# Third attention: the weighted products of two steps issued together

## What is computed

```python
q = (query @ Wq).reshape(b, sq, 32, 16).transpose(0, 2, 1, 3)
k = jnp.repeat((key @ Wk).reshape(b, sk, 8, 16).transpose(0, 2, 1, 3), 4, axis=1)
v = jnp.repeat((value @ Wv).reshape(b, sk, 8, 16).transpose(0, 2, 1, 3), 4, axis=1)
scores = jnp.einsum('bhqd,bhkd->bhqk', q, k) * 16 ** -0.5
probs = jax.nn.softmax(scores, axis=-1)
out = jnp.einsum('bhqk,bhkd->bhqd', probs, v)
x = x + jnp.tanh(g_xattn[2]) * (out.transpose(0, 2, 1, 3).reshape(b, sq, 512) @ Wo)
```

## Time and profile before

| | us |
|---|---|
| median of 3 runs | 1259.44 |
| lowest, highest | 1258.63, 1262.66 |
| profiled execution | 1258.08 |
| its span (first to last instruction) | 1256.3 |
| loop of the third attention (step 0 to last product) | 952.2 to 1058.9 of the span |

### The profile page before, as it was taken

How to read it: one execution, slowest core, us unless ns; L and a number is a source line. 1 busy time by engine, 2 the same in 40 slices (tenths; PEclk the granted TensorE clock), 3 DMA queues, 4 the chain that set the end, 5 groups by cost and what they waited for, 6 DMA issues and landing times.

```text
span 1256.3 us, 19440 instructions
## 1 busy us (share of the span) xinstructions
PE 1182.3 (94%) x7154; PEld 927.8 (74%) x7154; DVE 909.4 (72%) x1748; ACT 637.6 (51%) x1046; POOL 517.5 (41%) x385
## 2 busy tenths in 40 slices
PE   6999999999999998999989999997899998999986
PEld 5878888878888876777878879886775444777733
DVE  6589888886798798874677976897557773442287
ACT  3466556645566555641355644565146777232252
POOL 5126365625236377534242724234634002265212
PEclk9999999999999999999999999999999999999999
DMA  5588869975689597850386956878131000572000
GB/s 193 104 157 162 170 140 179 181 142 107 137 157 185 123 179 137 158 136 22 72 167 109 219 97 120 165 132 174 37 123 25 1 2 1 166 168 76 1 1 34
DMA packets 356238, 146.39 MB, mean 117 GB/s; under 512 B 327793, under 2 KB 334097, under 8 KB 356145
## 3 DMA queue, kind: packets, MB, share of 16 engines
q1 hardware_dynamic: 356144, 145.15, 55.3%
HBM read 57.17 MB, written 5.37 MB: 50 GB/s over the span
## 4 chain that ended last, share of the span: by engine, by line
PE 48%; DVE 9%; ACT 2%; POOL 2%; issue 2%; DMA 1%; SPq 0%; DVEq 0%; ACTq 0%; POOLq 0%
PE ps L876 6%; PE ps L2018 5%; PE ps L904 4%; PE ps L843 4%; PE ps L1584 3%; PE ps L1610 3%; DVE p L1166 3%; DVE rows_and_turned L1152 3%; PE ps L828 2%; PE ps L2031 2%; PE ps L819 2%; PE ps L805 2%; PE ps L2316 2%; PE ps L1566 1%; PE ps L1595 1%
## 5 line engine op out<-in xcount | busy, mean ns | idle before, releaser
L1000 ACT ACTIVATE ps<-ps,rows_and_turned 128x768 f32<-128x768 f32 x192 | 168.1, 875 | 201.5 <-DVE rows_and_turned L1152 201.5
L876 PE MATMUL ps<-kT,qT 128*128 128x512 f32 (+3 forms) x1152 | 238.9, 343 | 27.8 <-DVE p L1166 26.3
L876 PEld LDWEIGHTS ps<-kT,qT 128*128 128x128 f32 (+1 forms) x1152 | 199.2, 189 | 83.0 <-DVE p L1166 29.7
L1008 ACT ACTIVATE p<-ps,rows_and_turned 128x768 f16<-128x768 f32 x192 | 173.0, 901 | 125.2 <-ACT ps L1000 114.3
L904 PE MATMUL ps<-pT,vv 128*128 128x256 f16 (+1 forms) x1728 | 221.7, 274 | 6.2 <-issue 6.2
L1152 DVE TENSOR_REDUCE rows_and_turned<-ps 128x1 f32<-128x768 f32 x192 | 183.1, 954 | 56.8 <-PE ps L876 54.9
L1166 DVE SCALAR_TENSOR_TENSOR p<-ps,rows_and_turned,p 128x768 f16<-128x768 f32 (+2 forms) x256 | 201.4, 808 | 3.7 <-ACT p L1008 3.7
L904 PEld LDWEIGHTS ps<-pT,vv 128*128 128x128 f16 (+1 forms) x1728 | 167.3, 107 | 26.5 <-issue 9.6
L828 PE MATMUL ps<-xT,wq 128*128 128x512 f32 x528 | 144.0, 408 | 0.0
L737 POOL TENSOR_TENSOR wo<-raw,one 128x512 fp32r<-128x512 f32 (+1 forms) x48 | 50.8, 1058 | 225.2 <-PE ps L843 199.4
L1942 POOL TENSOR_TENSOR f2w<-f2raw,f2w 128x1024 fp32r<-128x1024 f32 (+2 forms) x33 | 52.6, 1622 | 149.2 <-ACT f2w L2062 149.2
(11 more groups left out here) (277 smaller groups left out, 1913.9 us busy)
## 6 DMA issues: line engine op xcount, KB each, us to landing
raw<-in_l_wq SPq DMA_DIRECT2D x44, 256.0 KB, 3.3
f2raw<-in_f_w SPq DMA_DIRECT2D x11, 776.0 KB, 5.0
rows_and_turned<-in_m_w SPq DMA_DIRECT2D x11, 768.0 KB, 5.6
raw<-in_l_wo SPq DMA_DIRECT2D x32, 256.0 KB, 3.3
pT<-p SPq DMA_TRANSPOSE x192, 3.7
raw<-in_l_wo SPq DMA_DIRECT2D x16, 192.0 KB, 3.3
w3gu<-rows_and_turned SPq DMA_DIRECT2D x11, 256.0 KB, 2.8
ctxraw<-in_ctxT SPq DMA_DIRECT2D x2, 1024.0 KB, 8.0
```

The lines of the kernel that those rows point to most:

```text
L876: last = nc.tensor.matmul(sc[:, lo:hi], query(A, h, qp)[:, r * P:(r + 1) * P], keys(A, h // A.g)[0:hd, kp, b, lo:hi], start=(qp, kp) == PA ...
L1000: nc.scalar.activation(score_banks(n), score_banks(n), ACT.Exp, bias=nmax[:, n % 32:n % 32 + 1], accum_out=rsum[:, n % 32:n % 32 + 1]).the ...
L1008: nc.scalar.activation(p16[:, n % 3, HI], score_banks(n), ACT.Copy, scale=rden[:, n % 32:n % 32 + 1]).then_inc(sem("att_half"), 1)
```

## The change

In odd steps no product is issued any more. In an even step n, from 2 on, both `weighted(n - 2)` and `weighted(n - 1)` are issued, one behind the other. The last two products, behind the loop, stay as they are, and so do the queues of all other engines, the buffers and the semaphores.

```diff
@@ -1673,8 +1673,9 @@
                     shifted(g + 1, 1, "l2_q4", 2 * g + 3)
                 if i == 7 and g + 2 < G2:
                     queries(g + 2, 1, "l2_q4", 2 * g + 4)
-                if n >= 2:
+                if n >= 2 and n % 2 == 0:
                     weighted(n - 2)
+                    weighted(n - 1)
             weighted(STEPS2 - 2)
             weighted(STEPS2 - 1)
             rows(G2 - 1, "l2_rows", G2 - 1)
```

## The result

| | before | changed |
|---|---|---|
| median of 22 runs each, us | 1260.74 | 1265.44 |
| span of the profiled execution, us | 1256.3 | 1264.6 |
| loop: first load of step 0 to first load of the last product | 952.18 to 1058.18 = 106.0 | 953.94 to 1065.59 = 111.65 |

The ratio is 1.0044, with a 95% interval of 1.0033 to 1.0054: 5.5 us slower, between 4.2 and 6.8; the two medians lie 4.7 apart. The loop alone is 5.65 us longer; the forecast was 5.8.

What follows compares the result with a forecast made beforehand. The prediction took the round trip of the two score banks as the bound, not TensorE's work. Terms of +3.2, +1.5, +0.6 and +0.5 made +5.8 us on the median 1259.44: 1265.2 us, range 1261.0 to 1269.5.

Steps and rivals of the forecast that it cites:

- first rival: TensorE's work is the bound: each of 31 pairs saves 0.14, nothing is given back, 1255.1 us; 6 in 100.
- empty step: Odd step i = 5, without product or tile: TensorE stands idle, the step lasting 1.35 us.
- round trip: A score's wait for its bank's earlier reduction: 0.54 + 0.69 + 0.12 = 1.35 us.
- Step (1): Product behind its neighbour in even steps: the second costs 0.43 instead of 0.57 us, a pair 1.00.
- third rival: Products don't stream in the loop, 0.57 + 0.57: 29 x 0.14 = 4.1 us more, 1269.3; 11 in 100.
- Step (2): Odd steps without a product: 1.35 us each, from start to start, with or without a tile.
- second rival: Odd steps' idle time comes back in even ones: 1259.4 us, or 1258 to 1261; 9 in 100.
- Step (3): Even steps, second score 0.59 late: 2.02 us at i = 0 and 2, 2.61 at 6, 2.81 at 4.
- wait for the output rows at i = 4: Tile at i = 4 waits for VectorE's output rows of i = 3, ending at 2.44: 0.20 us more.
- Step (4): Products' waits for exponentials: none while scores run, before step 53.
- output copy: ScalarE's copy holding up a group's first product: can start sooner, which gains nothing.
- saved switch: TensorE's saved change to another kind of tile, 0.14 us a pair; decides where no score waits for its bank.

Runs made afterwards that it cites:

- halved reductions: Reductions read 256 of 512 columns, in both kernels: kernel before 1249.57 us, changed kernel 1258.88 us, one run each, beside 1262.11 for the kernel before.
- the pairs in odd steps: Against the changed kernel, both products (n-3 and n-2) issued in odd steps, none in even ones: 1267.89 us, ratio 1.0062 to the kernel before.
- the product put back: Changed kernel with the pair of i = 4 undone, one product each at i = 4 and i = 5: 1265.63 us, one run.
- the moved products: Against the kernel before, products moved from steps that turn a tile to steps that don't, up to three in one: 1256.09 us, ratio 0.9972.

## Why the prediction was right

**The bound.** The argument that carried it was that a step costs the same with and without a product. Read by the busy share alone, would have given the first rival, and a gain. Halving the reductions confirms it: the engine with 21.0 us of idle time was part of the path. The changed kernel's empty step shows that it is there by the round trip (1.34, and 1.07 with halved reductions), not by its share of work.

**The number.** That the median came out at 1265.44 for a forecast of 1265.2 is in part luck. The forecast added 5.8 to a median of three runs, 1259.44; over 22 runs the kernel before has 1260.74. What can be held against the 5.8 is the loop's 5.65 and the ratio's 5.5.

**Step (1), the pair.** 1.00 from the pair's first load to the next score's, as the single pair at the end had shown. The third rival (no streaming behind a held score) is refuted by the row at 991.40 and its successor. It was priced at 29 pairs, without a word on which; 26 stand in steps with scores, and these would give 3.6 more instead of 4.1.

**Step (2), odd steps.** 1.34 with and without a tile, forecast 1.35. The second rival, that the hole is filled, is refuted by the empty step of 1.34 and by the pairs in odd steps.

**Step (3), even steps.** 2.02, 2.81, 2.61, 2.03 as forecast. The wait for the output rows at i = 4 was foreseen from VectorE's own order. Its multiplication is here:

```profile
1005.10 0.42 DVE L1814 TENSOR_TENSOR rows_and_turned<-ps,rden 128x256 f32<-128x256 f32 x1
```

It ends 2.44 into step 27 (1003.08), the number worked out.

**Step (4), waits.** While scores run, a product waited for an exponential only by what the view shows as 0.17 ahead of 991.40, which is the gap it also has where nothing holds it (996.24 to 996.83); the exponential of step 19, which that pair needs, had ended at 990.05. The output copy cost the step at i = 2 nothing beyond 0.01.

**The sum**, part by part:

| | forecast | loop of the trace |
|---|---|---|
| steps 2 to 8 | +1.5 | 13.03 - 11.54 = +1.5 |
| steps 9 to 48 | +3.2 | 74.16 - 71.04 = +3.1 |
| steps 49 to 52 | +0.6 | 7.53 - 6.92 = +0.6 |
| steps 53 to 63 | +0.5 | 13.85 - 13.43 = +0.4 |

The last part was an estimate and the least exact. Its pairs of steps lost 0.27, 0.43 and 0.19, where 0.2, 0.4 and 0.2 were estimated, and gained 0.34 and 0.15 instead of 0.14 each: the first one because two turned scores in a row load closer together than I had thought (below). Steps 0 and 1 are the same in both kernels within 0.01. That the 5.8 would be passed on in full is borne out by the ratio (5.5) as far as it can be: its interval, 4.2 to 6.8, is wider than the difference.

**What stays open.** The prediction calls the saved switch the mechanism that decides once no score waits for its bank. The kernel with halved reductions and pairs did not get there, as its step i = 5 still waits for the round trip.

## What to carry to other kernels

Where two engines hand work to each other through two banks, work out the round trip first, start of the producer to the bank's next use, and compare it with the time between these uses: what the producer's engine does inside the round trip is free, and what is moved out of it, into a step that is already longer than the round trip, is not. An engine's idle time proves nothing against its being on the path, and a high busy share proves nothing for it; a step that lacks the work in question, at a loop's start or end, is the best witness. Batching like work saves switches, 0.14 us each here, but first ask what each piece was filling.

## What the runs showed of the hardware

The changed kernel's first steps without scores, 53 and 54, as weight loads:

```profile
1051.74 0.30 PEld L1595 LDWEIGHTS ps<-q4T,k3T 64*128 64x128 f32 x4 [0.41 <-ACT q4T L1742]
1052.39 0.42 PEld L1566 LDWEIGHTS ps<-ident,qrow 128*128 128x128 f32 x4 [0.36 <-issue]
```

The four loads of two turned scores stand within 0.30 us, and the tile follows 0.65 after the first. One turned score takes 0.43 to the next load of another kind (1059.35 to 1059.78 in this kernel), two apart from each other 0.86; so two of one kind save 0.21, as a second product saves 0.14. A third product costs 0.43 again (24 loads at 1007.65, the next score 1.43 later). And I had not expected the timing to be so even: with durations read from a few groups, the steps of the pairs in odd steps, of the product put back and of the moved products came out within 0.02 us of what was worked out.
